# High and low filter taps side by side: one interleaved tap transfer for two in the spectral stage

## What is computed

```python
for i, frac in enumerate((1, 2, 4, 8)):
    xi = x[:, :T // frac]
    # 16 filters phi[:, k]: causal convolution over tokens, plain and with alternating signs,
    # each result mixed over channels by a 128 x 128 matrix
    si = einsum('btkd,k,kde->bte', U_plus, sigma**0.25, Mpp[i])
    si += einsum('btkd,k,kde->bte', U_minus, sigma**0.25, Mpm[i])
    si += sum over 3 lags of x shifted by the lag @ M_u[i]
    outs.append(pad(si))
out = sum(outs * weights)
```

## Time and profile before

| what | value |
|---|---|
| median of three runs | 7228.07 us (7223.17 to 7236.26) |
| profiled execution, its own time | 7226.66 us |
| its span | 7224.6 us |
| mean granted TensorE clock | 0.959 |
| first tap matmul to last | 4280.3 to 7185.8 us from the start |

### The profile page before, as it was taken

One profiled execution on the slowest core, in us unless ns is written; L12 is line 12 of the kernel. 1 busy time (PEld: TensorE's weight loads), 2 busy tenths in 40 slices (PEclk: granted clock), 3 DMA queues, 4 the chain that ended last, 5 costly groups with the idle time before them and its releaser, 6 DMA issues. The chain is left out here.

```text
span 7224.6 us, 134134 instructions
## 1 busy us (share of the span) xinstructions
PE 6403.4 (89%) x46555; PEld 5618.5 (78%) x46555; DVE 4389.0 (61%) x6035; ACT 3479.8 (48%) x7328; POOL 2750.0 (38%) x2143
## 2 busy tenths in 40 slices
PE   8798888988679888889875469999999899999998
PEld 4688787888348878778764349999999799999997
DVE  1799999999429999999975533333333333333333
ACT  2799999999239999999962111111111111111110
POOL 0588888888118888888850000000000000000000
PEclk9899999999789999999988779999999999999999
DMA  1122222222212222222221133333332233332323
GB/s 37 68 88 85 87 89 83 88 85 87 62 38 89 85 87 88 84 88 89 83 79 35 48 136 111 107 111 108 109 108 108 106 108 108 108 108 108 108 108 112
DMA packets 222967, 653.42 MB, mean 90 GB/s; under 512 B 22770, under 2 KB 112722, under 8 KB 189138
## 3 DMA queue, kind: packets, MB, share of 16 engines
q1 hardware_dynamic: 222114, 641.73, 25.0%
q10 hardware_dynamic: 576, 8.39, 0.3%
HBM read 618.30 MB, written 31.76 MB: 90 GB/s over the span
## 5 line engine op out<-in xcount | busy, mean ns | idle before, releaser
L1432 PE MATMUL p_conv<-window,x_high 128*128 128x256 f32 (+1 forms) x13824 | 2632.9, 293 | 54.5 <-DMA window<-taps_scratch 30.0
L607 POOL TENSOR_TENSOR read<-state,c_wide 128x1024 f32<-128x1024 f32 x1024 | 2435.2, 2378 | 461.3 <-DVE state L669 459.0
L1432 PEld LDWEIGHTS p_conv<-window,x_high 128*128 128x128 f32 x13824 | 2157.1, 189 | 243.4 <-issue 181.1
L669 DVE TENSOR_TENSOR_SCAN state<-decay,carry,p_drive 128x512 f32<-128x512 f32 x1792 | 2145.6, 1259 | 15.3 <-ACT decay L561 11.8
L1432 PE MATMUL p_conv<-window,x_low 128*128 128x256 f32 (+1 forms) x6912 | 1940.8, 281 | 0.0
L561 ACT ACTIVATE decay<-step,a_neg 128x512 f32<-128x512 f32 x2048 | 1416.6, 715 | 233.8 <-DVE state L669 233.5
L1432 PEld LDWEIGHTS p_conv<-window,x_low 128*128 128x128 f32 x6912 | 1308.6, 189 | 0.0
L454 PE MATMUL p_drive<-diag_b,xu_tok 128*128 128x128 f32 x8192 | 1106.0, 285 | 119.1 <-DVE state L669 115.4
L454 PEld LDWEIGHTS p_drive<-diag_b,xu_tok 128*128 128x128 f32 x8192 | 1011.2, 197 | 212.2 <-DVE state L669 152.0
L465 PE MATMUL p_y<-ident,read 128*128 128x128 f32 x8192 | 1072.5, 274 | 3.8 <-POOL read L607 3.8
L1512 ACT COPY filtered<-p_conv 128x512 f32<-128x512 f32 x128 | 75.1, 587 | 1935.6 <-PE p_conv L1432 1935.6
(11 more groups left out here) (233 smaller groups left out, 4662.6 us busy)
## 6 DMA issues: line engine op xcount, KB each, us to landing
c_wide<-c_scratch SPq DMA_DIRECT2D x256, 1024.0 KB, 4.7
window<-taps_scratch SPq DMA_DIRECT2D x256, 576.5 KB, 9.4
window<-taps_scratch SPq DMA_DIRECT2D x128, 640.5 KB, 4.9
window<-taps_scratch SPq DMA_DIRECT2D x128, 448.5 KB, 8.5
m_both<-in_M_plus SPq DMA_DIRECT2D x33, 256.0 KB, 2.9
m_both<-in_M_minus SPq DMA_DIRECT2D x33, 256.0 KB, 3.3
gate_scratch<-gate_out SPq DMA_DIRECT2D x16, 512.0 KB, 3.1
gate_in<-gate_scratch SPq DMA_DIRECT2D x16, 512.0 KB, 4.5
```

What stands on the lines that cost most here:

```text
L607: pool.tensor_tensor(read[:, n % 4, :, :], state[:, n % 4, :, :], wide, ALU.mult).then_inc(s["read_out"], 1)
L669: dve.tensor_tensor_scan(flip(state[:, n % 4, t, :], c), flip(decay[:, n % 2, t, :], c), flip(p_drive[:, n % 2, t, :], c), 0.0 if c.start ...
L1432: last = pe.matmul(o, x[:, source, blk + j, :], window[kind][v][z][:, end - width:end][:, ::-1], start=first, stop=True, skip_group_check= ...
```

## The change

The two parts of a tap become neighbours. `split` is laid out as (vector, tap, part), `taps_dram` as (vector, row, tap, part), and `window` has one tile for kind and vector with the part as the last index. VectorE writes each part with a step of two elements. A store carries both parts: 4 transfers of taps instead of 8, one of zeros instead of 2. A window is filled by 4 transfers for a kind instead of 8, each with rows twice as long. TensorE reads a part from the shared tile, so that successive columns lie 8 bytes apart instead of 4. The numbers of matmuls, weight loads and bytes are the same.

```diff
-        split = sb("taps_split", [P, 2, VECTORS, L], fp32r)
-        zero = sb("taps_zero", [KF, 2, PAD])
+        split = sb("taps_split", [P, VECTORS, L, 2], fp32r)
+        zero = sb("taps_zero", [KF, 2, PAD, 2])
...
-            for part in range(2):
-                sp.dma_start(m.taps_dram[0, part, :, HALF:HALF + PAD].rearrange("(k n) x -> k n x", n=2),
-                             zero[:, :, :]).then_inc(stored, 16)
+            sp.dma_start(m.taps_dram[0, :, HALF:HALF + PAD, :].rearrange("(k n) x h -> k n (x h)", n=2),
+                         zero[:, :, :, :].rearrange("k n x h -> k n (x h)")).then_inc(stored, 16)
...
             for q in range(4):
-                for part in range(2):
-                    dst = m.taps_dram[:, part, :, q * L:q * L + L].rearrange("v r x -> r v x")
-                    sp.dma_start(dst, split[32 * q:32 * q + 32, part, :, :].bitcast(fp32)).then_inc(stored, 16)
-            sp.wait_ge(stored, 16 * 10)
+                dst = m.taps_dram[:, :, q * L:q * L + L, :].rearrange("v r x h -> r v (x h)")
+                sp.dma_start(dst, split[32 * q:32 * q + 32, :, :, :].bitcast(fp32).rearrange("r v x h -> r v (x h)")
+                             ).then_inc(stored, 16)
+            sp.wait_ge(stored, 16 * 5)
...
-            dve.tensor_copy(split[:, 0, :, :], vec[:, :, :]).then_inc(high, 1)
+            dve.tensor_copy(split[:, :, :, 0], vec[:, :, :]).then_inc(high, 1)
             dve.wait_ge(high, 1)
-            dve.tensor_tensor(split[:, 1, :, :], vec[:, :, :], split[:, 0, :, :].bitcast(fp32),
+            dve.tensor_tensor(split[:, :, :, 1], vec[:, :, :], split[:, :, :, 0].bitcast(fp32),
                               ALU.subtract).then_inc(low, 1)
...
-        m.taps_dram = nc.dram_tensor("taps_scratch", [VECTORS, 2, KF * 2, HALF + PAD], fp32, kind="Internal").ap()
+        m.taps_dram = nc.dram_tensor("taps_scratch", [VECTORS, KF * 2, HALF + PAD, 2], fp32, kind="Internal").ap()
...
-        window = [[[sb(f"window{kind}{v}{part}", [P, TOP - FIRST[v]], fp32r) for part in range(2)]
-                   for v in range(VECTORS)] for kind in range(2)]
+        window = [[sb(f"window{kind}{v}", [P, TOP - FIRST[v], 2], fp32r) for v in range(VECTORS)] for kind in range(2)]
...
                         for v in range(VECTORS):
-                            for part in range(2):
-                                row = m.taps_dram[v, part][ds(k * 2 + kind, 1), :].rearrange("k x -> (k x)")
-                                sp.dma_start(window[kind][v][part][:, :].bitcast(fp32),
-                                             shifted_rows(row, HALF - TOP, TOP - FIRST[v])).then_inc(s[f"z{kind}"], 16)
+                            row = m.taps_dram[v][ds(k * 2 + kind, 1), :, :].rearrange("k x h -> (k x h)")
+                            sp.dma_start(window[kind][v][:, :, :].bitcast(fp32).rearrange("p x h -> p (x h)"),
+                                         shifted_rows(row, HALF - TOP, TOP - FIRST[v])).then_inc(s[f"z{kind}"], 16)
...
-                            last = pe.matmul(o, x[:, source, blk + j, :], window[kind][v][z][:, end - width:end][:, ::-1],
+                            last = pe.matmul(o, x[:, source, blk + j, :], window[kind][v][:, end - width:end, z][:, ::-1],
...
-                    pe.wait_ge(s[f"z{kind}"], START + n * 128 + 128)
+                    pe.wait_ge(s[f"z{kind}"], START + n * 64 + 64)
...
-    return bass.AP(tensor=row.tensor, offset=row.offset + first, ap=[[1, P], [1, width]])
+    return bass.AP(tensor=row.tensor, offset=row.offset + 2 * first, ap=[[2, P], [1, 2 * width]])
```

More of the change, by code:

```diff
@@ L1114, in _ @@
             sp.wait_ge(zeroed, 1)
-            sp.dma_start(raw[0:3 * NEAR].rearrange("(a x) -> a x", x=64), zero[0:12, 0, 0:64]).then_inc(raw_out, 16)
-            for part in range(2):
-                sp.dma_start(m.taps_dram[0, part, :, HALF:HALF + PAD].rearrange("(k n) x -> k n x", n=2),
-                             zero[:, :, :]).then_inc(stored, 16)
+            sp.dma_start(raw[0:3 * NEAR].rearrange("(a x) -> a x", x=64), zero[0:12, 0, 0:32, :].rearrange(
+                "a x h -> a (x h)")).then_inc(raw_out, 16)
+            sp.dma_start(m.taps_dram[0, :, HALF:HALF + PAD, :].rearrange("(k n) x h -> k n (x h)", n=2),
+                         zero[:, :, :, :].rearrange("k n x h -> k n (x h)")).then_inc(stored, 16)
             sp.wait_ge(kept, 16)
@@ L1161, in _ @@
             X = mybir.AxisListType.X
-            dve.memset(zero[:, :, :], 0.0).then_inc(zeroed, 1)
+            dve.memset(zero[:, :, :, :], 0.0).then_inc(zeroed, 1)
             dve.wait_ge(loaded, 64)
```

## The result

The changed kernel is slower: 9273.17 us, median of four runs (9271.71 to 9276.37), against 7231.31 us (7223.17 to 7236.26) for the kernel before, a ratio of 1.283 with a 95% interval of 1.281 to 1.285. That is the side forecast, inside the likeliest case's own range (8890 to 9330 us), 292 us above the 8981 us named. The range stated for all cases, 7220 to 9330 us, took in no change as well, so the range of the likeliest case is the sharper test.

The account below looks back on a forecast made before the run. TensorE's gapless tap matmuls were taken to bound the convolution stage. Profiled 7226.66 us, plus 1754 for the halved read rate, minus 1 for small edits, gave 8980, so 8981 us as the median; range 7220 to 9330 us.

Parts of the forecast that it names:

- likeliest case: Interleaved reads halve the rate of TensorE's wide tap matmuls: 8890 to 9330 us, chance 0.64.
- What bounds the stage: Convolution stage is a string of TensorE matmuls without gaps, count times pace: 2875 us reckoned against 2878.5 busy.
- TensorE's step: Tap matmuls reading columns 8 bytes apart: wide ones +99.3 ns each, +1754 us; narrow ones 0.
- 256 x 0.84 = 215: Wide tap matmul's interleaved read in ns, at plain fp32's 0.84 ns a column; 218 with an odd start's 3 ns.
- The two readings for a full reader: Adjacent reads already at the limit: 118 ns exceeds weight load (110) and stream (106.7); odd starts cost 2.7 ns more.
- The small terms: Edits outside TensorE's read, in transfers and VectorE's splitting: about -1 us together, between -8 and +5.
- The cast: VectorE's splitting instruction, writing every other element, slows to the subtraction's pace: +1.1 us.
- The stores: Uncovered stores of taps before the next part, with fewer issues: -1 us, between nothing and -4.1.
- the first windows: Uncovered first window transfers before the first matmul, with fewer issues: -1 us, between nothing and -3.7.
- The step is free: Rival: TensorE's 8-byte step costs nothing, leaving only the small edits: 7220 to 7233 us, chance 0.20.
- Only some of the reads suffer: Rival: say only odd starts, a quarter of the units, slow down: +437 us, 7665 us; chance 0.09.
- Faster: Rival: moving and stationary reads collide less over twice the address range: -154 us, 7073 us; chance 0.05.

Follow-up runs that it names:

- e1: Kernel before, but every tap matmul reads every other column (8 bytes apart) of one tap tile: 9286.55 us.
- e6: Changed kernel, but TensorE reads adjacent values of the shared interleaved tile: 7232.28 us, ratio 1.0002.
- e4: Kernel before, but each moving column is read twice in a row, so half as many different columns: 7105.12 us.
- e7: Kernel before, but moving columns are taken in runs of four neighbours, then four left out: 7632.24 us.
- e10: Kernel before, but each four columns are taken in the order 0, 2, 1, 3: 7235.40 us.
- e12: Kernel with two correction products in bf16, grouped by type, but with the bf16 tap parts side by side, columns 4 bytes apart: 7122.15 us.
- e9: Kernel before, but with two correction products in bf16 and each bank's fp32r products put first, then the bf16 ones: 7032.73 us, ratio 0.974.
- e2: Kernel before, but every tap matmul reads columns 16 bytes apart (a step of 4) of one tap tile: 9351.02 us.
- e3: Kernel before, but moving columns are taken as two neighbours, then two left out: 9174.06 us.
- e5: Changed kernel, but with the part as an outer index of the shared tile, so TensorE reads adjacent columns: 7247.35 us, ratio 1.0021.
- e11: Changed kernel with the part as an outer index and window rows padded by 3 values, so low taps begin at a 16-byte multiple: 7233.34 us, ratio 1.0009.

## Why the prediction was right, point by point

**What bounds the stage** was right: pace and counts give TensorE's time in it to 4 us, before and after.

**TensorE's step** was the deciding term, and it was named as such; e1 shows that it is the whole of the loss, e6 that nothing else is part of it. Its size was too small: I took 218 ns for a wide matmul and 110 for a narrow one, the runs gave 233.5 and 118. The difference, 15.5 x 17,664 + 8 x 3,072 = 274 + 25 = 299 us, is the miss. The mis-sized term is "256 x 0.84 = 215": I let the halved rate be that of streamed plain fp32 columns. Those are adjacent, and that their pace is near half the fp32r one says nothing of a read with a step. The limit is on the reading side and starts from the present 118 ns; doubling that gives 236, the upper end that I had kept for the range. The clock at 0.50 shows it: the same 233 ns. So the mechanism held, and it was the upper end, not the middle, that took in the measured time.

**The two readings for a full reader** led the right way, and both can now be told more exactly. That the 118 ns lie above weight load and stream was indeed the read: e4 takes half the bytes and falls to 112. That an odd start costs 2.7 ns fits the boundaries of 16 bytes in part: a slice of 256 adjacent values touches 64 pieces, one off 65, which would be 1.8 ns of the 2.7, at 118 / 64 = 1.84 ns a piece. No run tests that single piece. Where each run of four starts odd, as in e7, the rate falls to half. What was too coarse is "the interleaved read" as such: a step of 8 bytes costs nothing where the columns of a piece are all taken in turn (e10).

**The small terms** sum to nothing, as forecast (-1 us, between -8 and +5; e6 +1.9, with an interval of some 7 us to either side). The cast, for which I took +1.1 us, stayed at 1.23: VectorE writes every other element at no cost here. The stores gained 0.2 us and the first windows 0.75, for the -1 each that I took. Issue time set neither: the issues of the stores fell by 2.9 us for those 0.2. That bytes set them fits the DMA shares of the earlier trace rows, and no run varied the bytes.

**The rivals.** "The step is free" was wrong; it is free only where four successive columns need no more than one new piece (e10, and e12 to within the 6 ns that the read then sets). "Only some of the reads suffer" did not occur in this change, all units have 233.5 ns; but e7, with aligned and odd runs, is just that case, at 7632 us. "Faster", by fewer collisions, did not occur either. The 8.7 ns above the weight load can be had, by reading less (e4, and in part e9), not by spreading the addresses.

The Trainium skill, in "Advanced Engine Details and Errata", SBUF Cachelines, says that at least two hits on a 16-byte line are needed to absorb the latency of the memory; the prediction read that as enough. In this case two hits do not reach the full rate for TensorE's moving operand: with 8-byte steps, and with pairs of neighbours, there are two on each line, and the pace is 233.5 and 228.5 ns for 118. The lines of 16 bytes themselves show plainly, in e7; the measurement decides on the count, which is four for the fp32r columns here.

**What stays open.** With one new piece for four columns a piece takes 1.84 ns, with two it is 3.65 ns for the four columns; but with four (e2) only 3.72. So a price for each piece describes one and two, and what holds the price down beyond that was not found. The runs fit as well with another reading: where four columns need more than one new piece, each column costs about the same, 0.89 to 0.93 ns (e3, the change, e2, over 256 columns), however many pieces they touch. Nor is it shown why the paces of single products differ by some ns between e5 and e11.

## What to carry to other kernels

Before interleaving operands for the sake of fewer transfers, ask whether the transfer is on the path (here 62 waits of SyncE for TensorE said that it was not), and what the layout does to the innermost step of the engine that bounds the stage. For TensorE's moving operand, keep any four successive columns to one new 16-byte piece (shown here for fp32r, and for bf16 in e12); parts that must share a tile go in it as blocks, one behind the other (e5 and e11, within 17 us of the kernel before). Where a pace lies a few per cent above the weight load and the stream, suspect the read: narrower operands, grouped by type, were the change that did pay.

## What the hardware showed that was not expected

- A strided fp32r matmul of 256 columns takes 233 ns with the granted clock at 0.50 and at 1.00 alike; adjacent columns take 213 and 118.
- Columns 16 bytes apart cost hardly more than columns 8 bytes apart, 238 against 234 ns.
- Out of order within 16 bytes (0, 2, 1, 3) is free: 118 ns.
- One fp32r and two bf16 wide matmuls in turn take 353 to 358 ns together, hardly less than three of fp32r, though the bf16 ones take 110 each when grouped by type.
- VectorE's cast of 2048 values takes 1.23 us whether it writes adjacent values or every other one.
